# Splitting VectorE's additions of probabilities by head in a one-core attention and convolution kernel

## The reference

```python
num = H * W                      # 4096
hd = C // NUM_HEADS              # 32, 8 heads
q = proj(Wq, bq) / math.sqrt(hd)
k = proj(Wk, bk)
v = proj(Wv, bv)
attn = jax.nn.softmax(jnp.einsum('bnd,bmd->bnm', q, k), axis=-1)
fuse = jnp.einsum('bnm,bmd->bnd', attn, v)
```

## Time and profile before

| | us |
|---|---|
| median of three runs (4297.22 to 4299.57) | 4298.28 |
| the profiled execution, its own time | 4293.3 |
| its span in the trace | 4291.3 |
| TensorE busy in the span | 4042.1 |
| VectorE busy | 3617.7 |
| GpSimd busy | 3536.1 |
| ScalarE busy | 2450.8 |
| one unit of attention | 53.5 |

### The profile page before, as it was taken

How to read it: one execution, slowest core, us unless ns; L and a number is a source line. 1 busy time by engine, 2 the same in 40 slices (tenths; PEclk the granted TensorE clock), 3 DMA queues, 4 the chain that set the end, 5 groups by cost and what they waited for, 6 DMA issues and landing times. The chain is left out here.

```text
span 4291.3 us, 82398 instructions
## 1 busy us (share of the span) xinstructions
PE 4042.1 (94%) x20277; PEld 1972.5 (46%) x20277; DVE 3617.7 (84%) x5250; ACT 2450.8 (57%) x4584; POOL 3536.1 (82%) x1552
## 2 busy tenths in 40 slices
PE   7979999999999999999999999999999999877766
PEld 4534444444444444444444444444444444333322
DVE  3379999999899999998999999999999999377988
ACT  1216666666566666665666666666666666524344
POOL 3439999999889999998899999999999999846566
PEclk9959999999999999999999999999999999988888
DMA  6931100110011001100110011001100000030201
GB/s 194 284 85 39 40 20 21 41 40 20 20 41 40 20 21 41 40 20 21 41 40 20 21 41 40 20 21 41 40 20 21 21 20 17 7 94 15 74 20 39
DMA packets 213798, 184.92 MB, mean 43 GB/s; under 512 B 115986, under 2 KB 140740, under 8 KB 213316
## 3 DMA queue, kind: packets, MB, share of 16 engines
q1 hardware_dynamic: 213508, 181.74, 15.8%
HBM read 122.10 MB, written 59.24 MB: 42 GB/s over the span
## 5 line engine op out<-in xcount | busy, mean ns | idle before, releaser
L759 ACT ACTIVATE prob<-st 128x512 f32<-128x512 f32 x4096 | 2154.3, 602 | 1307.3 <-PE st L624 1049.1
L817 DVE TENSOR_REDUCE block_max<-mx 128x1 f32<-128x512 f32 x4096 | 2562.8, 683 | 340.7 <-PE mx L631 327.3
L488 POOL TENSOR_TENSOR prob_sum<-prob_sum,prob 128x1024 f32<-128x1024 f32 x768 | 1928.8, 2511 | 126.9 <-POOL prob_sum L488 95.3
L631 PE MATMUL mx<-keys,max_queries 96*128 96x512 f32 x4096 | 1647.9, 426 | 38.0 <-DMA keys<-k_scratch 27.6
L624 PE MATMUL st<-queries,keys 97*128 97x512 f32 x4096 | 1576.2, 411 | 1.4 <-ACT prob L759 1.3
L488 POOL TENSOR_TENSOR prob_sum<-prob 128x1024 f32<-128x1024 f32 x448 | 1066.8, 2381 | 251.9 <-ACT prob L759 251.9
L631 PEld LDWEIGHTS mx<-keys,max_queries 96*128 96x128 f32 x4096 | 778.4, 191 | 733.3 <-DVE block_max L817 562.5
L643 PE MATMUL acc<-prob,values 128*32 128x512 f32 x8192 | 1038.7, 602 | 0.0
L624 PEld LDWEIGHTS st<-queries,keys 97*128 97x128 f32 x4096 | 777.8, 190 | 520.7 <-ACT prob L759 283.6
L1200 POOL TENSOR_TENSOR conv<-conv,weighted_pixels 128x512 f32<-128x512 f32 x192 | 315.4, 1674 | 204.9 <-DVE conv L1258 121.3
L643 PEld LDWEIGHTS acc<-prob,values 128*32 128x32 f32 x8192 | 194.6, 109 | 426.9 <-issue 226.4
(11 more groups left out here) (122 smaller groups left out, 1426.9 us busy)
## 6 DMA issues: line engine op xcount, KB each, us to landing
max_queries<-q_scratch SPq DMA_DIRECT2D x384, 64.0 KB, 1.9
queries<-q_scratch SPq DMA_DIRECT2D x384, 64.0 KB, 1.9
keys<-k_scratch SPq DMA_DIRECT2D x168, 128.0 KB, 2.5
x<-in_x SPq DMA_DIRECT2D x18, 512.0 KB, 4.2
q_scratch<-high SPq DMA_DIRECT2D x32, 256.0 KB, 4.2
k_scratch<-high SPq DMA_DIRECT2D x16, 512.0 KB, 4.9
q_scratch<-low SPq DMA_DIRECT2D x32, 256.0 KB, 5.0
k_scratch<-low SPq DMA_DIRECT2D x16, 512.0 KB, 5.0
```

Source lines behind the costliest of these rows:

```text
L488: ops.tensor_tensor(psum[k][:, :, :], a[:, :, :], prob[(first + i) % RING][:, :, :], ALU.add).then_inc(added[own], 1)
L631: nc.tensor.matmul(mx[bank(j, p)][:, :], qm[p][:, h, ns * P:(ns + 1) * P], kk[gp][0:SPLIT, h, blk * CH:(blk + 1) * CH], start=True, stop=T ...
L759: nc.scalar.activation(prob[s % RING][:, h, :], st[bank(i, p)][:, :], ACT.Exp).then_inc(exp_done, 1)
L817: nc.vector.tensor_reduce(bmax[p][:, j // MB, j % MB:j % MB + 1], mx[bank(j, p)][:, :], AX.X, ALU.max).then_inc(mx_taken, 1)
```

## The change

VectorE's three additions a unit become six, each of one head: 128 x 512 elements, with the same operands otherwise. They stand after maxima 42, 44, 49, 51, 53 and 55, where the three stood after 43, 51 and 54. The first half of each addition waits for the first head's exponential only. The counts of the semaphore `added` for VectorE's group are doubled, and a half of addition 2 or 3 waits for the half before it of its own head. GpSimd's additions and TensorE's `ORDER` are as they were.

```diff
-ADD_AFTER = [43, 51, 54]
+ADD_AFTER = [42, 44, 49, 51, 53, 55]
@@ def adds_until(k, i):
-    return sum(GROUPS[j] - 1 for j in range(k) if (j in BY_VECTOR) == same) + i
-
-ADDS = {vector: sum(g - 1 for k, g in enumerate(GROUPS) if (k in BY_VECTOR) == vector) for vector in (True, False)}
+    return (2 if same else 1) * (sum(GROUPS[j] - 1 for j in range(k) if (j in BY_VECTOR) == same) + i)
+
+ADDS = {vector: (2 if vector else 1) * sum(g - 1 for k, g in enumerate(GROUPS) if (k in BY_VECTOR) == vector)
+        for vector in (True, False)}
@@ def attention_phase
-        def add(engine, ops, u, k, i):
+        def add(engine, ops, u, k, i, heads=slice(0, 2)):
             if i == 1:
                 engine.wait_ge(sums_done, SUMS * u + k // 2 + 1)
             else:
-                engine.wait_ge(added[own], ADDS[own] * (u + 1) + adds_until(k, i - 1))
-            engine.wait_ge(exp_done, TILES * (u + 1) + 2 * (first + i) + 2)
+                engine.wait_ge(added[own], ADDS[own] * (u + 1) + adds_until(k, i - 1) - (2 - heads.stop))
+            engine.wait_ge(exp_done, TILES * (u + 1) + 2 * (first + i) + heads.stop)
             a = prob[first % RING] if i == 1 else psum[k]
-            ops.tensor_tensor(psum[k][:, :, :], a[:, :, :], prob[(first + i) % RING][:, :, :],
+            ops.tensor_tensor(psum[k][:, heads, :], a[:, heads, :], prob[(first + i) % RING][:, heads, :],
                               ALU.add).then_inc(added[own], 1)
@@ def _(dve):
-            additions = [(k, i) for k in BY_VECTOR for i in range(1, GROUPS[k])]
+            additions = [(k, i, h) for k in BY_VECTOR for i in range(1, GROUPS[k]) for h in range(2)]
@@ def between
-                for at, (k, i) in zip(ADD_AFTER, additions):
+                for at, (k, i, h) in zip(ADD_AFTER, additions):
                     if prev and j == at:
-                        add(dve, nc.vector, v - 1, k, i)
+                        add(dve, nc.vector, v - 1, k, i, slice(h, h + 1))
```

## The result

The changed kernel takes 4583.69 us (median of four runs, 4578.37 to 4589.10) where the kernel before takes 4298.48: a ratio of 1.0667, 95% interval 1.0652 to 1.0681. It is 285 us slower. The forecast was 4401, and its range ended at 4420.

What follows compares the result with a forecast made beforehand. TensorE's order of products was taken as the bound. A lost port race costing 1.64 + 0.1 = 1.75 us in 59 units adds 103 us to 4298.28, forecasting 4401; stated range 4290 to 4420, the forecast's own 4381 to 4418.

Steps and rivals of the forecast that it cites:

- The added semaphore steps: VectorE's extra semaphore work beside the running maximum: costed at nothing, at worst some 0.1 us three times a unit.
- Fifth and sixth: Halves after maxima 53 and 55: each waits about 1.1 us and ends 0.54 behind GpSimd; largest product lag some 0.1.
- I take it that GpSimd goes first: At maximum 42, GpSimd's addition starts 0.02 us ahead of VectorE's first half and takes the port; chance 0.45.
- rival (b): At maximum 42 either engine comes first, varying unit by unit: 4330 to 4385 us; chance 0.15.
- What a lost first half costs: After maximum 42: product 48 waits 1.64 us for maximum 45, plus 0.1 at product 57; 1.75 us a unit.
- Prices of a half: A 128x512 VectorE addition takes 0.68 us free, or ends 0.54 us after the GpSimd operation it waits behind.
- rival (c): After maximum 49 the third half also comes behind GpSimd; 1.3 us a unit reaches TensorE, 4483 us; chance 0.05.
- Rival (a): At maximum 42 VectorE gets the port first; 0.1 us a unit gained, 4292 us, own range 4275 to 4298; chance 0.35.
- the 0.36 of TensorE's wait: TensorE's stalls between product 47 and the value products, 3.03 less 2.67 us; removing all would give 4275.
- ScalarE behind VectorE's additions: ScalarE reusing the added tiles' buffers, exponentials 40 to 47: no wait expected, at worst 1.0 us a unit (63 us).
- The sign: Whole kernel: the change was expected to make it slower, with chance 0.63.

## Why the prediction was wrong

- **"The added semaphore steps are register work and I cost them at nothing."** This is the step that failed. Their own time was indeed not to be seen, but with the three halves they are instructions that have to be loaded, 16 more in a loop of 293, and the loop no longer came round without a load: 30 turns of 7.0 us, 209 of the 282. Nothing in the sum stood for the loading of code, and no row of the kernel before shows how close its loop is to a bad place. The shortened loop (4416 instead of 4584 with the same additions) and the moved one (4446 instead of 4298 with no change of additions) show it from both sides.
- **"Fifth and sixth: each waits about 1.1."** Right for the fifth (1.67 long). The sixth was mis-sized: it comes 0.01 behind GpSimd's addition, waits for all of it, and takes 2.92. I had put a mean in place of the time at which it arrives, which I had worked out for each of the first four. It made the units 46 us longer than before, and in the run with the sixth half after 57 the units with a won race lost this and 0.2 each more.
- **"I take it that GpSimd goes first."** Wrong in 50 of 64 units. My half came where I had put it, 0.10 behind the end of exponential 26. What moved is the rival: GpSimd's addition starts 0.12 behind that end in the won units (median), not the 0.08 of the kernel before, with GpSimd's idle of 0.16 before it as ever; why it moved no run shows. The rule read from the earlier trace rows held, and more sharply than I knew: whoever starts first has the port, down to some 0.01 us. (In the shortened kernels five halves that start 0.001 to 0.002 behind still win; below that the start doesn't tell.) I carried a lead of 0.02 from one trace into another in which both engines' times are changed. This was rival (b), both orders.
- **What a lost first half costs.** 1.64 and 0.1 us were predicted; 2.3 were left over in the sum, and in the run with the sixth half after 57 such units take 1.9 more at the least and 4.5 and 5.1 in the medians. In the units where TensorE's clock did not fall the price is 1.9 to 2.2 (the two of the changed kernel without a turn, 56.38 and 56.46, and the nine above), near the 1.75 predicted. The rest is what the prediction did not have: a loss there also makes the later halves late, and they meet `fuse` and the addition behind it, and in the dearer units of that run TensorE's granted clock falls to 0.50 for a stretch.
- **Prices of a half.** 0.68 free, 0.54 behind GpSimd's end: measured 0.68 to 0.69 and 0.55. The second took 1.67 (predicted 16.75 to 18.42, the same), the fourth 1.72, the third 0.68 in nearly every unit; rival (c) did not come.
- **Rival (a), per unit.** VectorE first was to gain 0.1 a unit and not the 0.36 of TensorE's wait. The won units without the other two costs gain 0.2. (The 0.36 itself is 0.40 by its own terms: ten steps of 0.23 and 0.33 are 2.63, not 2.67.) The rule named there, of the Trainium skill's page "Perfetto Trace Analysis", section "Optimizing Scalar/DVE Operations", that breaking up instructions may let work be done sooner, came out for these units and not for the kernel.
- **ScalarE behind VectorE's additions,** costed at nothing: it waited for them six times, 11.8 us in all, and not once in the kernel before.
- The sign was right, but the reason given for it, the lost first half, was about a tenth of the loss (27 of 282).

What stays open: why GpSimd's start moved from 0.08 to 0.12, and why the race is lost in 14 units of one kernel and 25 of another (each counted in one traced execution, and the executions of the shortened kernels differ by up to 72 us); how much of a lost race is TensorE's clock; and the rule of good and bad places for a loop, which fits all thirteen kernels, but with a starting place that was fitted to them.

## What to carry to other kernels

Before an edit adds instructions to a hardware loop, look at how long the loop is on that engine, every wait and register step counted, and compare the packets of the instruction queue before and after, and look at the first instruction of a turn for an idle time "issue" afterwards; it can cost more than anything that the edit does. Where two engines share a port, cutting an instruction in two doubles the number of times it can be blocked, so work out the arrival of every piece, not of most, and try first to move the whole instruction to a place where the other is nearly done. A race that is decided by hundredths of a microsecond belongs into the range with both outcomes, since every edit moves both runners.

## What the runs showed of the hardware

- At the branch back of VectorE's loop, loading of code made it idle 2.9 us in the mean (kernel before, moved by 24: 85.9 us in 30) and 3.9 in the changed kernel (116.8 in 30). TensorE, which waited, lost 4.9 and 7.0 us a turn; three packets of the instruction queue came in the 5 us behind a turn in the changed kernel, two in the moved one, none in the kernels without stalls. Part of the difference goes with TensorE's clock: over the 62 units its mean granted clock was 0.98 in the moved kernel and 0.96 in the changed one.
- The port goes to whoever starts first, with 0.01 us enough (won and lost first halves of the changed kernel split by the sign of the lead). A waiting VectorE is served when GpSimd goes from one addition to the next with 0.16 of idle between, and also when `fuse` comes straight behind an addition (in the kernel with the first addition after 45 the one of 1128.52 is 1.60 long, and ends 1.09 behind GpSimd's addition, while `fuse` takes 2.26). But when GpSimd went from `fuse` straight into an addition, it was not served: 3.51 and 4.14 us for a half of 0.68.
- VectorE does not keep the port from one instruction to the next: with two halves one behind the other GpSimd's waiting addition came between them in nearly every pair, and the second took 2.85.
